# Two table slots combined on GpSimd instead of stored, a read and a masked copy moved forward in a four-layer chain

## What is computed

```python
def reference(x, ids0, len1, ids2, len3, ...):
    x = x + einsum('bct,bcd->bdt', x, W[ids0])          # stage 0: one of 16 matrices per batch
    x = x + mask(len1) * (conv(x, K1) + x * D1)         # layer 1: long convolution along time
    x = x + (x @ weight.T + bias + scale * low_rank)    # layer 2: 1024 x 1024 along time, one of 8 adapters
    x = x + mask(len3) * (conv(mask(len3) * x, K3) + mask(len3) * x * D3)   # layer 3
    return x

def kernel_of(log_dt, C, log_A_real, A_imag):           # K1 and K3, one row of 1024 per channel
    dtA = (-exp(log_A_real) + 1j * A_imag) * exp(log_dt)[:, None]
    Cs = C * (exp(dtA) - 1) / A
    return 2 * einsum('hn,hnl->hl', Cs, exp(dtA[:, :, None] * arange(1024))).real
```

## Time and profile before

| | us |
|---|---|
| median of 3 runs | 1604.87 |
| lowest and highest | 1602.5, 1608.54 |
| the profiled execution | 1609.9 |
| its span in the trace | 1608.1 |
| mean granted TensorE clock of it | 0.978 of full speed |

### The profile page before, as it was taken

How to read it: one execution, slowest core, us unless ns; L and a number is a source line. 1 busy time by engine, 2 the same in 40 slices (tenths; PEclk the granted TensorE clock), 3 DMA queues, 4 the chain that set the end, 5 groups by cost and what they waited for, 6 DMA issues and landing times.

```text
span 1608.1 us, 36825 instructions
## 1 busy us (share of the span) xinstructions
PE 1508.5 (94%) x14983; PEld 1305.9 (81%) x14983; DVE 1246.4 (78%) x1525; ACT 743.8 (46%) x1084; POOL 546.5 (34%) x260
## 2 busy tenths in 40 slices
PE   7787776989999999999999999999999999999998
PEld 6677775778888888888888888888888888888887
DVE  7878786979595969696878787887878686969563
ACT  4444443435454535354545454545444454545443
POOL 2111103473333333333333334343434343434030
PEclk9889889999999999999999999999999999999999
DMA  7799996558575765658574757483848484857432
GB/s 225 259 323 377 339 370 223 131 119 196 131 187 139 172 153 153 173 129 192 126 191 121 193 119 204 107 219 89 225 95 214 90 229 96 223 104 210 111 132 67
DMA packets 455255, 287.63 MB, mean 179 GB/s; under 512 B 331528, under 2 KB 410896, under 8 KB 453072
## 3 DMA queue, kind: packets, MB, share of 16 engines
q1 hardware_dynamic: 405904, 174.57, 46.5%
q10 hardware_dynamic: 49216, 110.98, 19.8%
HBM read 161.30 MB, written 75.96 MB: 148 GB/s over the span
## 4 chain that ended last, share of the span: by engine, by line
PE 66%; DVE 19%; DMA 6%; issue 5%; ACT 3%; ACTq 0%; SPq 0%; DVEq 0%
PE ps L899 27%; PE ps L803 8%; PE ps L987 6%; DMA arena<-in_x_dram 5%; PE ps L876 5%; PE ps L908 4%; PE ps L847 4%; PE ps L751 3%; DVE arena L1793 3%; PE ps L1000 3%; PE ps L813 3%; DVE arena L1848 3%; DVE arena L1805 2%; DVE lowd L1885 2%; PE ps L687 1%
## 5 line engine op out<-in xcount | busy, mean ns | idle before, releaser
L899 PE MATMUL ps<-arena,w2t 128*128 128x256 f16 x4608 | 525.4, 273 | 17.2 <-ACT arena L1320 14.0
L899 PEld LDWEIGHTS ps<-arena,w2t 128*128 128x128 f16 x4608 | 450.1, 98 | 77.5 <-issue 17.6
L618 POOL TENSOR_TENSOR arena<-arena 128x1024 f32<-128x1024 f32 x31 | 78.3, 2525 | 796.7 <-DVE arena L1855 430.2
L1898 DVE TENSOR_TENSOR arena<-arena 128x512 f16<-128x512 f32 x128 | 104.3, 815 | 126.0 <-ACT arena L1333 126.0
L1333 ACT ACTIVATE arena<-arena 128x512 f16<-128x512 f32 x128 | 80.6, 630 | 253.7 <-DVE arena L1894 252.7
L751 PE MATMUL ps<-arena 128*128 128x128 f32 x1024 | 147.7, 309 | 51.5 <-DMA arena<-in_x_dram 26.4
L751 PEld LDWEIGHTS ps<-arena 128*128 128x128 f32 x1024 | 139.7, 221 | 57.0 <-DMA arena<-in_x_dram 28.1
L1320 ACT ACTIVATE arena<-ps,biasx 128x256 f32<-128x256 f32 x256 | 103.3, 470 | 85.5 <-PE ps L908 51.3
L847 PE MATMUL ps<-arena 128*128 128x512 f16 (+1 forms) x768 | 136.9, 329 | 5.6 <-DVE arena L1793 5.6
L987 PE MATMUL ps<-arena 128*128 128x256 f16 (+1 forms) x1536 | 137.1, 246 | 2.6 <-DVE gbuf L1800 2.6
L987 PEld LDWEIGHTS ps<-arena 128*128 128x128 f16 x1536 | 122.0, 98 | 16.5 <-DVE gbuf L1800 6.3
(11 more groups left out here) (253 smaller groups left out, 2718.4 us busy)
## 6 DMA issues: line engine op xcount, KB each, us to landing
w2t<-w_scratch ACTq DMA_DIRECT2D x96, 512.0 KB, 3.9
arena<-in_x_dram SPq DMA_DIRECT2D x64, 512.0 KB, 8.1
out_dram<-arena SPq DMA_DIRECT2D x64, 512.0 KB, 3.4
gbuf<-x_scratch SPq DMA_DIRECT2D x120, 256.0 KB, 4.3
gbuf<-w_scratch ACTq DMA_DIRECT2D x32, 512.0 KB, 3.9
arena<-krow_scratch SPq DMA_DIRECT2D x31, 512.0 KB, 9.3
x_scratch<-arena ACTq DMA_DIRECT2D x14, 1024.0 KB, 10.7
x_scratch<-arena ACTq DMA_DIRECT2D x14, 896.0 KB, 7.7
```

Of the source, the lines that this page charges most:

```text
L899: mm = nc.tensor.matmul(ps[:, bank, n * HW:(n + 1) * HW], weight(p, n, part, k), xx[:, :, k, :], start=(fresh and n == 0 and k == 0 and q ...
L1898: tt(x3_quarter(x3l, h0, row), x3part[slot].rearrange("p (k h b) -> p k h b", k=2, h=2), x3_quarter(x3h, h0, row), ALU.subtract).then_inc( ...
```

## The change

- `NLEFT` goes from 4 to 2. Left slots 2 and 3 are no longer made by DVE nor stored. A group's row in tab_scratch has 2 x 68 + 2 x 64 numbers and, at its end, the two parts of the factor (2 x 4), so 272 numbers in place of 400. The loads per group are two of 68 KB.
- `combine_b` loses its six instructions and gets one copy of 32 numbers per partition.
- `make_tables` begins with six GpSimd instructions over 68 numbers per partition, which make slots 2 and 3 beyond the end of the loaded row. There are four waits on GpSimd's own semaphore `left_parts` among them and behind them.
- ACT: in all groups but the first, `read_part` stands ahead of quarter 0's split. In group 0 the split stays ahead of it. Of the halves of x1 the third stands behind both, the fourth behind `read_part` of bank 1 and quarter 1's split.
- DVE: `past_sum(g, 0)` moves from ahead of the first `x2_split_lo` to behind the third masked copy, and `past_sum(g, 1)` from behind the third copy to behind the fourth.

```diff
-NLEFT, NRIGHT = 4, 2
+NLEFT, NRIGHT = 2, 2
 LEFT = HG * TL
-TAB = NLEFT * LEFT + NRIGHT * HG * TB
+TAB = NLEFT * LEFT + NRIGHT * HG * TB + 2 * HG
...
+                re, im = [tab_now[:, TAB - (2 - k) * HG:TAB - (1 - k) * HG].rearrange("p (h o) -> p h o", o=1).to_broadcast([P, HG, TL])
+                          for k in range(2)]
+                l0, l1, l2, l3, tmp = [left_row(tab_now, k) for k in range(5)]
+                ptt(l2, l0, re, ALU.mult).then_inc(left_parts, 1)
+                ptt(tmp, l1, im, ALU.mult).then_inc(left_parts, 1)
+                ptt(l3, l1, re, ALU.mult).then_inc(left_parts, 1)
+                pool.wait_ge(left_parts, 6 * n + 3)
+                ptt(l2, l2, tmp, ALU.add).then_inc(left_parts, 1)
+                pool.wait_ge(left_parts, 6 * n + 4)
+                ptt(tmp, l0, im, ALU.mult).then_inc(left_parts, 1)
+                pool.wait_ge(left_parts, 6 * n + 5)
+                ptt(l3, l3, tmp, ALU.subtract).then_inc(left_parts, 1)
+                pool.wait_ge(left_parts, 6 * n + 6)
                 ptt(m4, left_of(tab_now, 2), right_of(tab_now, 0), ALU.mult).then_inc(u_parts, 1)
...
-                split_hi3(g, 0, 0, 0, 0)
+                if early:
+                    split_hi3(g, 0, 0, 0, 0)
+                read_part(g, 0, SUM_AT[0], 6, 0, 4, 5)
+                if not early:
+                    split_hi3(g, 0, 0, 0, 0)
                 if more1:
-                    for h in X1_ORDER[2:4]:
-                        x1_split_hi(g + 1, h)
-                read_part(g, 0, SUM_AT[0], 6, 0, 4, 5)
+                    x1_split_hi(g + 1, X1_ORDER[2])
+                read_part(g, 1, SUM_AT[1], 6, 0, 4, 6)
                 split_hi3(g, 1, 0, 2, 1)
-                read_part(g, 1, SUM_AT[1], 6, 0, 4, 6)
+                if more1:
+                    x1_split_hi(g + 1, X1_ORDER[3])
...
                 tmp = four(left_tmp)
-                tt(left_slot(r, 2), left_slot(r, 0), param(c, 2, TL), ALU.mult)
-                table_link(tt(tmp, left_slot(r, 1), param(c, 3, TL), ALU.mult), c, 15)
-                table_link(tt(left_slot(r, 2), left_slot(r, 2), tmp, ALU.add), c, 16)
-                tt(left_slot(r, 3), left_slot(r, 1), param(c, 2, TL), ALU.mult)
-                table_link(tt(tmp, left_slot(r, 0), param(c, 3, TL), ALU.mult), c, 17)
-                table_link(tt(left_slot(r, 3), left_slot(r, 3), tmp, ALU.subtract), c, 18)
+                nc.vector.tensor_copy(tab[r][:, :, TAB - 2 * HG:TAB].rearrange("p q (n r) -> p n q r", n=2),
+                                      turned[:, 2:4, bass.ds(c * CH, CH)].rearrange("p n (q r) -> p n q r", q=HG))
...
                     take_conv1(g + 1, 1)
-                    past_sum(g, 0)
                     x2_split_lo(g + 1, 0)
                     take_conv1(g + 1, 2)
-                    past_sum(g, 1)
+                    past_sum(g, 0)
                     x2_split_lo(g + 1, 1)
                     take_conv1(g + 1, 3)
+                    past_sum(g, 1)
```

More of the change, by code:

```diff
@@ L180, in build @@
         u32_first = part_of(gbuf, 36, 4).rearrange("p (h t) -> p h t", h=HG)
-        tab_first = w2t[:, 0, 3].rearrange("p s k o -> p (s k o)").bitcast(F32)[:, 0:TAB]
+        tab_first = w2t[:, 0, 3].rearrange("p s k o -> p (s k o)").bitcast(F32)
         g1n_first = w2t[:, 1:3, 3].rearrange("p q s k o -> p q (s k o)").rearrange("p q (m t) -> p q m t", t=CHUNK)
@@ L187, in build @@
         ut1 = area(80, 4, F16).rearrange("p (s m n) -> p s m n", s=2, m=2 * HG)
-        tabs = [area(84 + 2 * v, TAB / 256) for v in range(2)]
+        tabs = [area(84 + 2 * v, 2) for v in range(2)]
         x3l = area(88, 8, F16).rearrange("p (h k b) -> p h k b", h=HG, k=NBLK)
@@ L300, in build @@
         v_parts = sem("v_parts")
+        left_parts = sem("left_parts")
         v_made = sem("v_made")
@@ L317, in build @@
         ssm = (ssm1, ssm3)
-        NLINK = 19
+        NLINK = 15
         LOT_A, LOT_B, LOT_W = 0, 1, 2
@@ L591, in _, with left_row @@
             ptt = nc.gpsimd.tensor_tensor
+            def left_row(tab, n):
+                at0 = n * LEFT if n < NLEFT else TAB + (n - NLEFT) * LEFT
+                return tab[:, at0:at0 + LEFT].rearrange("p (h a) -> p h a", a=TL)
             def left_of(tab, n):
-                t = tab[:, n * LEFT:(n + 1) * LEFT].rearrange("p (h a) -> p h a", a=TL)
+                t = left_row(tab, n)
                 return t[:, :, 0:TB].rearrange("p h (a o) -> p h a o", o=1).to_broadcast([P, HG, TB, TB])
@@ L1646, in combine_b @@
                 tmp = four(left_tmp)
[L1647 to L1652 removed]
+                nc.vector.tensor_copy(tab[r][:, :, TAB - 2 * HG:TAB].rearrange("p q (n r) -> p n q r", n=2),
+                                      turned[:, 2:4, bass.ds(c * CH, CH)].rearrange("p n (q r) -> p n q r", q=HG))
                 tt(four(left_k)[:, :, :, ::-1], left_slot(r, 0), param(c, 4, TL), ALU.mult)
[L1654 removed]
+                table_link(tt(tmp, left_slot(r, 1), param(c, 5, TL), ALU.mult), c, 15)
                 tt(four(left_k), four(left_k), tmp[:, :, :, ::-1], ALU.add).then_inc(tables_ready, 1)
```

1 line of the change is left out of this document (removed).

## The result

| | before | after |
|---|---|---|
| median (us) | 1605.14 of 4 runs (1602.5 to 1608.54) | 1587.78 of 4 runs (1586.13 to 1593.22) |
| ratio to before | | 0.9897, 95% interval 0.9866 to 0.9927 |
| profiled execution, its span (us) | 1609.9, 1608.1 | 1593.2, 1591.4 |
| start of layer 1 (first PE block 128x512) | 258.14 | 255.12 |
| first group's end (loop begins) | 375.62 | 372.48 |

The kernel is 17.4 us faster, where 20.5 were forecast (1584.4; the range was 1574 to 1598). The two spans differ by 16.7 us. Of these 3.1 were won ahead of the loop and 13.5 in it. So the sum came out nearly as written, but its parts did not: the loop gave more than its share (12 forecast), and what lies ahead of it far less (8.5 forecast).

The account below looks back on a forecast made before the run. PE was taken to bound the loop (busy 81.77 of 82.75 us per group), with stage 0 another regime of busy DMA engines. -14.0 - 6 + 2 - 2.5 = -20.5 us gave a median of 1584.4 us, range 1574 to 1598.

Parts of the forecast that it names:

- Part 1: ACT's earlier read of the partial sum in the loop saves PE 1.00 us in each of 14 groups, -14.0 us.
- A rival: The loop does not get shorter: something else, such as bank 1's weights, is late near the read; 1597 to 1600, chance 0.08.
- that PE waits in the loop for anything new: Sign of being wrong: PE in the loop groups has a wait it did not have before; no size given.
- Part 2: Stage 0: smaller stores save 5.2 us by bytes, DVE 2.5 us per chunk, mostly hidden; -6 taken, bounds 2 and 10.
- Part 3: Six short GpSimd instructions start the table 2.2 us later; DVE's fourth masked copy 0.15 us later per group, +2 us.
- The walk: Loop timeline of DVE waiting for GpSimd's instruction in flight: third copy just in time, fourth ends at 1111.6, before 1111.45.
- Its other branch: At the loop's masked copies, with past sums not moved, the later GpSimd table would make it 1.2 us worse.
- The bound for a start 3.7 us later: At the loop's masked copies, a GpSimd table starting 3.7 us later makes the loss grow by 1.5 us.
- Part 4: Group 0: the eighth chunk's 2.5 us of DVE work leave the chain to PE's read wait; -2.5, bounds 0 and -3.5.
- group 1 starting less than 5 us earlier: Sign of being wrong about the time won ahead of the loop, in stage 0 and group 0.
- The copies in time: Rival: masked copies no longer late, -4.3 in place of +2, and stage 0 follows DVE at -9: 1575, chance 0.13.

Follow-up runs that it names:

- e1: Kernel before with only ACT's order changed, the partial sum read ahead of x1's halves; ratio 0.9918 to before, median 1593.6 us.
- e3: Kernel before with both ACT's and DVE's orders of the change, tables stored in full and made on DVE as before; ratio 0.9891, median 1588.1 us.
- e6: The change with stored rows of 400 numbers as before, 128 of them unused; ratio 0.9913 to before, median 1592.6 us.
- e7: The change with four more short GpSimd instructions of 68 numbers per table, each with its wait; ratio 1.0004 to before, median 1608.9 us.
- e5: The change with DVE's six old instructions per chunk of stage 0 done again as spare work; ratio 0.9887 to before, median 1589.0 us.
- e4: The change's tables alone, with ACT's and DVE's orders as before; ratio 1.0062 to before, median 1617.8 us.
- e2: Kernel before with only DVE's order changed, past sums moved behind the third and fourth masked copies; ratio 0.9978, median 1604.0 us.
- e12: The change's orders and three further moves as in e11, but tables stored in full and made on DVE as before; ratio 0.9881, median 1589.1 us.
- e8: The change with the first past sum also moved, so both stand behind the fourth masked copy; ratio 0.9862 to before, median 1585.0 us.
- e11: The change with the moves of e8, e9 and e10 together; ratio 0.9862 to before, median 1586.1 us.
- e9: The change with group 0's seventh load of weights issued ahead of the first table's split; ratio 0.9878 to before, median 1590.7 us.
- e10: The change with ACT's wait for the eighth table's store put behind the read in group 0; ratio 0.9884 to before, median 1589.0 us.

## Why the prediction was right, and where it was not

**Part 1 (-14.0) was right**, mechanism and size: e1 won 0.99 us per group and 13 us in all. What was to be late next was not: the third added sum is done at 1061.93 with 5.3 us in hand (7 were named). A rival was touched: a load of weights for bank 1 stopped PE in one to three groups of seven kernels that read early, by 0.2 to 1.2 us at most (0.4 in the trace of the change), and in none of the other seven (e1, e3, e6 and e7 among them, which read early too). What makes it late in some executions only is open. By the letter it is one of the prediction's signs of being wrong, that PE waits in the loop for anything new.

**Part 2 (-6) had the right cause and too large a size.** The bytes set stage 0's pace: the fourteen starts of layer 1 give 4.0 us, the executions of e5 and e6 some 3.5, and the pair of profiles 3.0. The sum by bytes was 5.2, which 4.0 with a doubt of 2 us does not exclude; the step that failed is the rounding up from it, which gave DVE's time a share. In e5, which starts layer 1 at 250.2 us with DVE's old work, no such share is seen. A single transfer's time says nothing here about its size: stores of 544 KB landed after 10.9 us from one buffer and 9.9 from the other (medians of four and three), those of 800 KB after 9.4 and 10.9.

**Part 3 (+2) was mis-sized by 3 us, on the good side.** Undisturbed short instructions of 0.29 to 0.33 us (0.32 forecast) are as forecast, and so is DVE's stop for the instruction in flight. The first of a table, at 0.82 us, is over the 0.45 that the prediction named as a sign of being wrong, and the table's main part starts 2.5 us later at the copies, a bit more than the 2.2 forecast. The walk put the loss at the fourth copy at 0.48 us and it is 0.26, so 13 x 0.07 = 0.9 us won where 2 were to be lost. The walk rested on margins of some 0.1 us and this is what it can give. Its other branch, 1.2 us worse with the past sums unmoved, was too small at the place: e4 lost 2.26 us per group against PE's own time, of which 0.33 were there before, so 1.9 more. But its time came out better than by that sum, since the stop at the read vanished under it (e4) just as it had grown under a gain (e2). The prediction added stops along one engine, and in two of the three experiments with one part alone they were not additive. For the whole change the sum came out because the read's stop went first.

The bound for a start 3.7 us later, 1.5 us more per group than before, was too high: e7 starts 4.1 us later and loses 1.30 us of PE's own 81.43, where before 0.33 were lost at the copies, so 0.97 more. That a DVE instruction with both inputs in SBUF doesn't run beside one of GpSimd's is seen in the fences of the change and of e4 at the copies: it ends 1.07 or 1.08 us after GpSimd's, where it takes 1.21 alone. This agrees with what the Trainium skill (SBUF — State Buffer, SBUF: two separate sides) says of the shared pair of ports, a lock held for the whole instruction, and the doubt it cast on this change was justified: by e3 the new tables cost 3.5 us in the loop and win about as much ahead of it. The change without them is as fast (0.9891).

**Part 4 (-2.5) failed.** Group 0 takes 117.4 us, where it took 117.5. The prediction followed the chain through DVE, booked its 2.5 us, and let GpSimd's first table end where it had ended, "nothing is won or lost by that". Counted from the start of layer 1 that table ended after 61.5 us before and ends after 62.6 now: it starts 1.3 us earlier, not 2.5, and its short instructions take 3.0 us, not 2.2. The second table, which comes at once behind it, was not followed; it takes 21.4 us, where it took 19.8. And GpSimd was on the path already before, as PE's, GpSimd's and DVE's timelines of before show:

```profile
323.22 2.79 PE L899 MATMUL ps<-arena,w2t 128*128 128x256 f16 x24 [0.58 <-DMA w2t<-w_scratch]
...
334.85 2.68 POOL L628 TENSOR_TENSOR arena<-arena 128x1024 f32<-128x1024 f32 x1
337.50 2.03 POOL L632 TENSOR_TENSOR arena<-twin,arena 128x512 f32<-128x512 f32 x1
...
335.24 3.37 DVE L1775 SCALAR_TENSOR_TENSOR arena<-arena 128x1024 f16<-128x1024 f32 x1
```

PE stood for the load that ACT issues once GpSimd's first table is done, and DVE's split of 335.24 stood for GpSimd's instruction of 334.85 (3.37 us in place of 1.21). Only the end of the second table, at 339.53, lay beside the chain: DVE's next split began at 339.91. These are the places relative to the start of layer 1, in us. The last column is PE's block L831 (L813 in the old code), which in every row but that of e7 begins 0.10 us behind DVE's instruction L1800 (L1782), whose result it uses:

| kernel | first table starts | second table ends | ACT splits it | PE's block L831 |
|---|---|---|---|---|
| before | 43.7 | 81.4 | 84.9 | 85.9 |
| e3, e12 (old tables) | 43.6, 43.7 | 81.3, 81.4 | 84.8, 84.9 | 85.9, 86.0 |
| the change | 42.4 | 84.1 | 84.8 | 86.0 |
| e8 to e11 | 42.4 to 42.6 | 84.7 to 84.9 | 84.7 to 85.0 | 85.9 to 86.2 |
| e5, DVE's old work | 45.0 | 86.6 | 87.4 | 88.5 |
| e7, ten short ones | 42.7 | 88.2 | 88.2 | 90.4 |

DVE's saving is there: the tables start 1.3 us earlier than before, and 2.6 earlier than with DVE's old work. But they end 2.7 to 3.5 us later. PE's block doesn't use the second table; it feels it through DVE. In e8 to e11, and in e4 and e6, the block begins 1.25 us behind GpSimd's end, in all six alike, because DVE's split stands until then (see e9); before it began 4.55 us behind it. That margin is used up, and so the block stands at 85.9 to 86.2 us in all of them, whatever stop was taken out on the way (e9, e10). In the change it begins 1.85 us behind. There GpSimd held DVE one step earlier on the same chain: the split of 332.60 took 2.95 us in place of 1.21. e7 adds 4.4 us at this block, and e5, which gives DVE its work back, 2.5. (In e1 and e2, which have the old code there, the first table started 1.3 us later than before and the block 1.8 later, so a comparison of two single executions is good to some 2 us; that of the rows within one is sharper.) Of what would make it wrong the prediction had named this: group 1 starting less than 5 us earlier. It started 3.1 us earlier.

**The sum** was right to 3 us partly by luck: part 3's error, 3 in favour, met those of parts 2 and 4, 3 and 2.5 against; with three groups of the trace that were 0.6, 0.3 and 0.2 us longer than the rest (one of them by the late load) the 16.7 us are complete. The rivals: none came as written. "The copies in time" is what e8 is, not the change.

## What to carry to other kernels

Before adding up the stops of one engine, ask of each what releases it: if it is another engine's chain, a gain ahead of it is paid back there, and a loss can be hidden by it. Work moved from one busy engine to another one on the same chain won nothing in group 0 here, however short the instructions were; find where that chain is one after the other (here a table that begins when the last chunk is done) and book both ends. Where two engines exclude each other, the cheapest cure is often to take an unhurried instruction out from between two urgent ones, as e8 does.

## What the runs showed of the hardware that was not expected

GpSimd's instruction of 68 numbers per partition, 0.29 us alone, took up to 3.3 us (group 0 of the change, at 318.08) while DVE's instructions ran one behind another: the stop works in both directions, and is longest for the shortest instruction, relative to what it does. In stage 0, with the DMA engines busy for 0.99 of the time, a store of two thirds the size did not land clearly sooner (10.9 and 9.9 us by buffer, where the full one took 9.4 and 10.9). And the loop repeats to 0.03 us but for one to three groups, while stage 0, at the DMA engines' limit, scatters by 6 us between executions: for the one a single profile is enough, for the other only the means of several tell 4 us from nothing.
